# Routed experts of the second half of the tokens, computed only where they are chosen

## The reference, cut to what matters

```python
for e in range(2):                                  # shared experts, all tokens
    shared_out += (silu(x @ s_w1[e].T) * (x @ s_w3[e].T)) @ s_w2[e].T
s = sigmoid([x, t] @ W_router.T)                    # 8 scores per token
topk_idx = top_k(s + bias, 2)                       # 2 of 8 experts
gates_full = ...                                    # zero for 6 of 8 experts
for e in range(8):                                  # routed experts, hidden size 128
    routed_out += gelu(x @ r_w1[e].T) @ r_w2[e].T * gates_full[:, e:e+1]
out = (shared_out / 2 + routed_out) / 4
```

## Time and profile before

| | us |
|---|---|
| median of 3 runs | 550.57 (550.49 to 550.91) |
| span of the profiled execution | 549.0 |
| TensorE busy | 535.7 (98%) |
| VectorE busy | 430.2 (78%) |
| ScalarE busy | 380.4 (69%) |
| GpSimd busy | 197.6 (36%) |
| DMA traffic | 37.35 MB |

### The profile page before, as it was taken

The page is one execution under the profiler, slowest core; times in us unless marked ns, Lnnn a source line. Parts: engine busy times, 40 slices in busy tenths (PEclk is TensorE's granted clock), DMA queues, the critical chain, the costliest instruction groups (busy, mean ns, idle before and its releaser), DMA issues.

```text
span 549.0 us, 10031 instructions
## 1 busy us (share of the span) xinstructions
PE 535.7 (98%) x3309; PEld 464.1 (85%) x3309; DVE 430.2 (78%) x1042; ACT 380.4 (69%) x857; POOL 197.6 (36%) x186
## 2 busy tenths in 40 slices
PE   8999999999999999999999989999999999999997
PEld 7877888887877899999999877789999999987785
DVE  4987655676868888668756259989999999999866
ACT  5567767768766755344553256988988888888965
POOL 4688788888788203939000000010000000000100
DMA  8634305521090302030000000111111111111211
GB/s 290 192 153 159 153 4 229 193 111 44 1 338 11 135 4 80 0 117 21 1 1 0 1 1 1 27 32 21 20 19 22 20 31 35 36 36 41 49 50 38
DMA packets 30226, 37.35 MB, mean 68 GB/s; under 512 B 20096, under 2 KB 23648, under 8 KB 29280
## 3 DMA queue, kind: packets, MB, share of 16 engines
q1 hardware_dynamic: 30176, 36.72, 20.8%
HBM read 30.24 MB, written 2.28 MB: 59 GB/s over the span
## 4 chain that ended last, share of the span: by engine, by line
PE 80%; DVE 13%; ACT 3%; issue 2%; POOL 2%; DVEq 0%; ACTq 0%
PE bank L325 10%; PE bank L1264 10%; PE bank L326 10%; PE bank L327 10%; PE bank L1689 4%; PE bank L1775 4%; PE bank L1679 4%; PE bank L1716 3%; PE bank L1717 3%; PE bank L1332 2%; PE bank L1214 1%; POOL hidden_low L387 1%; PE bank L1764 1%; PE bank L1802 1%; PE bank L1788 1%
## 5 line engine op out<-in xcount | busy, mean ns | idle before, releaser
L387 POOL TENSOR_TENSOR hidden_low<-hidden,hidden_high 128x512 fp32r<-128x512 f32 x72 | 94.5, 1320 | 21.5 <-ACT hidden_high L372 19.3
L2070 POOL CAST h_high<-h 128x256 fp32r<-128x256 f32 x15 | 6.4, 426 | 197.5 <-ACT h L1881 191.1
L468 ACT ACTIVATE bank<-bank 128x512 f32<-128x512 f32 x56 | 32.6, 583 | 30.4 <-PE bank L327 30.1
L472 DVE TENSOR_TENSOR hidden<-bank,big 128x512 f32<-128x512 f32 x56 | 38.5, 687 | 14.3 <-ACT bank L468 13.3
L372 ACT CAST hidden_high<-hidden 128x512 fp32r<-128x512 f32 x70 | 43.1, 615 | 4.4 <-DVE hidden L472 3.1
L325 PE MATMUL bank<-xin_high,sw_high 128*128 128x256 f32 x128 | 43.9, 343 | 0.0
L1716 PE MATMUL bank<-taps_high,q1T 128*128 128x512 f32 x94 | 42.8, 456 | 1.0 <-ACT q1T L1844 0.6
L1717 PE MATMUL bank<-taps_low,q1T 128*128 128x512 f32 x94 | 37.1, 395 | 0.0
L1817 ACT ACTIVATE gates_t<-bank,lstm_b_half 128x128 f32<-128x128 f32 x96 | 28.2, 364 | 12.1 <-PE bank L1689 8.8
L1398 DVE COPY yT<-bank 128x256 f32<-128x256 f32 x32 | 13.5, 423 | 28.9 <-PE bank L1264 28.9
L1679 PE MATMUL bank<-x,lstm_wx 128*128 128x128 f32 x256 | 34.4, 277 | 1.7 <-ACT gates_t L1817 0.9
(11 more groups left out here) (274 smaller groups left out, 1734.8 us busy)
## 6 DMA issues: line engine op xcount, KB each, us to landing
big<-gates_scratch SPq DMA_DIRECT2D x7, 2048.0 KB, 7.6
w<-in_f_w SPq DMA_DIRECT2D x16, 256.0 KB, 5.9
onehot<-topi_scratch SPq DMA_DIRECT2D x8, 512.0 KB, 4.0
outT<-x SPq DMA_DIRECT2D x15, 128.0 KB, 2.1
xT<-in_xT SPq DMA_DIRECT2D x3, 512.0 KB, 6.9
hidden<-in_ffn_w SPq DMA_DIRECT2D x3, 256.0 KB, 5.3
hidden<-in_conv_w SPq DMA_DIRECT2D x3, 256.0 KB, 4.4
xT<-in_xT SPq DMA_DIRECT2D x2, 256.0 KB, 4.0
```

What stands on the lines that cost most here:

```text
L387: pool.tensor_tensor(hidden_hl[u % 3][1][:, :], hidden[u % 3][:, :], hidden_hl[u % 3][0][:, :].bitcast(F32), ALU.subtract).then_inc(s_lo, 1)
L472: dve.tensor_tensor(hidden[u % 3][:, :].rearrange("p (i k) -> p i k", k=P), r_bank[j % 2][:, :].rearrange("p (i k) -> p i k", k=P), gate_r ...
```

## The change

The number of dense chunks becomes 4 (`DENSE`): chunks 0 to 3 are as before. Chunks 4 to 7 (tiles 16 to 31, 2048 tokens, 4096 token-expert pairs) get the shared experts alone, from four new programs `shared_pe`, `shared_act`, `shared_dve` and `shared_sp`; in these the low part of the hidden tile and of x is made on VectorE instead of GpSimd. The pairs of the router are sorted by expert into slots: within chunks 2 and 3 VectorE and TensorE count and place them by prefix sums (`slot_counts` to `slots_experts`), each expert's share filled up to whole tiles of 128 slots, at most `SPARSE_TILES` = 39. GpSimd writes the 4096 rows of x to their slots in DRAM with 32 indirect DMAs (`scatter_pool`), 128 rows of 512 bytes each. Then a new stage, here called the sparse stage, takes the 39 tiles in 13 trios: SyncE reads each tile's expert number from SBUF into a register and loads that expert's two weight matrices by it (`load_weights`), and the trio's rows (`load_xs`); TensorE transposes, and multiplies in plain f32 (`sparse_turn`, `sparse_up`, `sparse_down`, 136 columns since the gate scores are made with the same matmul from weights prepared by `routed_gate_weights`); the results go back to DRAM by slot (`store_y`). Buffers: 5 trios of weights and rows, 2 of results. At last GpSimd fetches the two result rows of each token with 32 further indirect DMAs (`gather_pool`), and VectorE adds them, times the gate, to tokens and scores (`combine`) in the groups 0 and 1 of stage C, 16 instructions a chunk.

Around it: the choice of half 1 becomes two quarters (`CHOICES`), made at the ends of groups 0 and 1, after the combines. The gather of group 0's tokens, `weight_sums` and the first expert splits move from chunk 7 and group 0 into the sparse stage. `prepare_weights` stays behind `gather_pool` in GpSimd's program. Chunk 2 also issues DMAs of 1 MB (rows of x), 2.5 MB (a first fill of the slots, DRAM to DRAM) and 1 MB (weights, DRAM to DRAM). No gate rows are loaded for chunks 4 to 7.

The constants, and what `chunk` issues beside its units in chunks 2 and 3:

```diff
+HALF = NTILE // 2
+PAIRS_ROUTED = HALF * P * 2
+SPARSE_TILES = PAIRS_ROUTED // P + E - 1
+TRIO = 3
+TRIOS = SPARSE_TILES // TRIO
+W_SPARSE = 2 * P + E
+YROW = P + E
...
+        if c == 2 and u == 11:
+            slots_counted()
+        if c == 3 and u == 0:
+            slots_based()
+        if c == 3 and u == 1:
+            slots_placed()
+        if c == 3 and u == 3:
+            slots_gated()
+        if c == 3 and u == 4:
+            slots_experts()
+        if c == 3 and u == 11:
+            store_gate_weights()
+    if c == 2:
+        load_gate_rows(3, 1)
+        sp.dma_start(x_rows[:, :], t["x_rows"]).then_inc(s_rows, 16)
+        some = t["xT"].rearrange("p (a b) -> (p a) b", b=C)
+        sp.dma_start(xs_dram[0:TOK, :], some).then_inc(s_rows, 16)
+        sp.dma_start(xs_dram[TOK:SPARSE_TILES * P, :], some[0:SPARSE_TILES * P - TOK, :]).then_inc(s_rows, 16)
+        sp.dma_start(wcat[:, :, 0:2 * P], t["r_cat"]).then_inc(s_wcat, 16)
+    if c == 3:
+        sp.wait_ge(s_gg, 3 * NRO)
+        sp.dma_start(rw2_rows, t["r_w2"]).then_inc(s_gw, 16)
```

The slots and the shared chunks (`shared_act` does the tanh and the high parts of `chunk`'s ScalarE program, one unit apart):

```diff
+def slot_counts():
+    pe.wait_ge(s_sce, 2)
+    pe.wait_ge(s_id, BEFORE_READY)
+    chosen_rows = rank[:, HALF:NTILE, :].rearrange("p i e -> p e i")
+    for k, w in enumerate((before, ones[:, :])):
+        mm = pe.matmul(by_expert(acc_bank[1][:, k * P:(k + 1) * P]), w, chosen_rows, start=True, stop=True)
+    mm.then_inc(s_side, 1)
...
+def slots_placed():
+
+    first_of = by_expert(scan)[:, :, 0:1].rearrange("p e o -> p (e o)")
+    dve_pos(dve.tensor_tensor(shift, shift, first_of, ALU.subtract))
+    dve_pos(dve.tensor_tensor(scan, scan, earlier, ALU.add))
+    dve_pos(dve.tensor_tensor(by_expert(scan), by_expert(scan),
+                              shift.rearrange("p (e o) -> p e o", o=1).to_broadcast([P, E, HALF]), ALU.add))
+    dve_pos(dve.tensor_tensor(by_tile(placed), by_tile(scan), rank[:, HALF:NTILE, :], ALU.mult))
+    dve_pos(dve.tensor_reduce(pair_at[:, 1, :], by_tile(placed), X, ALU.max))
+    dve_pos(dve.tensor_reduce(pair_at[:, 0, :], by_tile(placed), X, ALU.add))
+    dve_pos(dve.tensor_tensor(pair_at[:, 0, :], pair_at[:, 0, :], pair_at[:, 1, :], ALU.subtract))
+    dve.tensor_copy(slot_at[:, :, :], pair_at).then_inc(s_sided, 1)
...
+def routed_gate_weights():
+    pe.wait_ge(s_sce, 3)
+    pe.wait_ge(s_gw, 32)
+    for e in range(E):
+        mm = pe.matmul(acc_bank[0][:, e * E:(e + 1) * E], rw2_rows[:, e * P:(e + 1) * P], gate_w[:, :],
+                       start=True, stop=True)
+    mm.then_inc(s_side, 1)
...
+def shared_up(k):
+    c, j = k // NSH, k % NSH
+    if j == 0:
+        pe.wait_ge(s_xs, 2 * c + 2)
+    if k < FIRST_SHARED + 2:
+        pe.wait_ge(s_q, k - 1)
+    elif k == FIRST_SHARED + 2:
+        pe.wait_ge(s_gg, DENSE * NRO)
+    else:
+        pe.wait_ge(s_q, k - 2)
+    for b, w in zip(shared_pair(k), (sw1_hl, sw3_hl)):
+        product(b[:, :], w, slice(j * P, (j + 1) * P), x_hl[c % 2], True, True).then_inc(s_ab, 1)
...
+        pe.wait_ge(s_dc, TURNED)
+    pe.wait_ge(s_lo, v + 1)
+    product(acc_bank[c % 2][:, :], sw2_hl, slice(j * P, (j + 1) * P), hidden_hl[v % 3],
+            j == 0, j == NSH - 1).then_inc(s_down, 1)
...
+def shared_silu(k):
+    v = shared_number(k)
+    dve.wait_ge(s_th, k + 1)
+    dve.scalar_tensor_tensor(pb[k % 2][:, :], th[k % 2][:, :], 1.0, shared_pair(k)[0][:, :],
+                             ALU.add, ALU.mult).then_inc(s_p, 1)
+    dve.wait_ge(s_p, k + 1)
+    dve.wait_ge(s_ab, 2 * k + 2)
+    dve.wait_ge(s_lo, v - 2)
+    dve.tensor_tensor(hidden[v % 3][:, :], pb[k % 2][:, :], shared_pair(k)[1][:, :], ALU.mult).then_inc(s_q, 1)
...
+def shared_low(k):
+    v = shared_number(k)
+    dve.wait_ge(s_hi, v + 1)
+    dve.wait_ge(s_lo, v)
+    dve.tensor_tensor(hidden_hl[v % 3][1][:, :], hidden[v % 3][:, :], hidden_hl[v % 3][0][:, :].bitcast(F32),
+                      ALU.subtract).then_inc(s_lo, 1)
...
+def shared_dve():
+    for k in range(FIRST_SHARED, LAST_SHARED):
+        c, j = k // NSH, k % NSH
+        shared_silu(k)
+        if k > FIRST_SHARED:
+            shared_low(k - 1)
+        if j == 0 and c + 1 < NCHUNK:
+            shared_x_low(c + 1)
+        if j == 0 and c > DENSE:
```

The indirect writes and SyncE's program:

```diff
+def scatter_pool():
+    pool.wait_ge(s_sided, SLOTS_READY)
+    pool.wait_ge(s_rows, 48)
+    for i in range(HALF):
+        for r in range(2):
+            pool.indirect_dma_start(xs_dram[:, :], bass.IndirectOffsetOnAxis(slot_at[:, r, i:i + 1], 0),
+                                    x_rows[:, i * C:(i + 1) * C], None).then_inc(s_scat, 16)
...
+def load_weights(m):
+
+    if m >= RING:
+        sp.wait_ge(s_sd, m - RING + 1)
+    for k in range(TRIO * m, TRIO * (m + 1)):
+        e = sp.value_load(tile_expert[0:1, k:k + 1], min_val=0, max_val=E - 1)
+        sp.dma_start(w_ring[k % (RING * TRIO)], wcat[ds(e, 1), :, :].rearrange("o p k -> (o p) k")
+                     ).then_inc(s_trio[m % RING], 16)
...
+def load_xs(m):
+
+    if m >= RING:
+        sp.wait_ge(s_xt, m - RING + 1)
+    rows = xs_dram[m * TRIO * P:(m + 1) * TRIO * P, :].rearrange("(j p) c -> p j c", j=TRIO)
+    sp.dma_start(xs[m % RING].rearrange("p (j c) -> p j c", j=TRIO), rows).then_inc(s_trio[m % RING], 16)
...
+def store_y(m):
+    sp.wait_ge(s_yv, m + 1)
+    rows = ys_dram[m * TRIO * P:(m + 1) * TRIO * P, :].rearrange("(j p) c -> p j c", j=TRIO)
+    sp.dma_start(rows, y_out[m % 2].rearrange("p (j c) -> p j c", j=TRIO)).then_inc(s_yst[m % 2], 16)
...
+    for c in range(DENSE, NCHUNK):
+        load_expert(c)
+    sp.wait_ge(s_wcat, 32)
+    sp.wait_ge(s_gg, DENSE * NRO)
+    sp.wait_ge(s_sided, EXPERTS_READY)
+    for m in range(RING):
+        load_weights(m)
+    choice_store(0)
...
+def sparse_sp():
+    sp.wait_ge(s_scat, 16 * 2 * HALF)
+    sp.wait_ge(s_down, DENSE_UNITS)
+    for m in range(RING):
+        load_xs(m)
+    sp.wait_ge(s_vc, 32)
+    for k in range(2):
+        gather_loads(0, k)
+    load_slots(0)
+    load_raw_weights()
+    for m in range(TRIOS):
+        if m + RING < TRIOS:
+            load_xs(m + RING)
+            load_weights(m + RING)
+        store_y(m)
```

The sparse stage, the indirect reads and the sum:

```diff
+def sparse_turn(m):
+    pe.wait_ge(s_trio[m % RING], TRIO_LOADED * (m // RING + 1))
+    if m < 2:
+        pe.wait_ge(s_q, LAST_SHARED)
+    else:
+        pe.wait_ge(s_xc, m - 1)
+    for j in range(TRIO):
+        mm = pe.transpose(bank[m % 2][:, j * P:(j + 1) * P], xs[m % RING][:, j * P:(j + 1) * P], ident[:, :])
+    mm.then_inc(s_xt, 1)
...
+def sparse_up(m):
+    pe.wait_ge(s_xc, m + 1)
+    if m >= 2:
+        pe.wait_ge(s_sg, m - 1)
+    for j in range(TRIO):
+        w = w_ring[(TRIO * m + j) % (RING * TRIO)]
+        mm = pe.matmul(bank[4 + m % 2][:, j * P:(j + 1) * P], w[:, 0:P], x_cols[m % 2][:, j * P:(j + 1) * P],
+                       start=True, stop=True)
+    mm.then_inc(s_su, 1)
...
+def sparse_down(m):
+    pe.wait_ge(s_sg, m + 1)
+    if m >= 2:
+        pe.wait_ge(s_yv, m - 1)
+    for j in range(TRIO):
+        w = w_ring[(TRIO * m + j) % (RING * TRIO)]
+        mm = pe.matmul(bank[2 + (m + 1) % 2][:, j * YROW:(j + 1) * YROW], hid[m % 3][:, j * P:(j + 1) * P],
+                       w[:, P:W_SPARSE], start=True, stop=True)
+    mm.then_inc(s_sd, 1)
...
+def sparse_pe():
+    sparse_turn(0)
+    sparse_turn(1)
+    sparse_up(0)
+    for m in range(TRIOS):
+        if m + 2 < TRIOS:
+            sparse_turn(m + 2)
+        if m + 1 < TRIOS:
+            sparse_up(m + 1)
+        sparse_down(m)
...
+def sparse_gelu(m):
+    act.wait_ge(s_su, m + 1)
+    if m >= 3:
+        act.wait_ge(s_sd, m - 2)
+    act.activation(hid[m % 3], bank[4 + m % 2][:, 0:TRIO * P], ACT.Gelu).then_inc(s_sg, 1)
...
+def sparse_y(m):
+    act.wait_ge(s_sd, m + 1)
+    if m >= 2:
+        act.wait_ge(s_yst[m % 2], 16 * (m // 2))
+    act.copy(y_out[m % 2], bank[2 + (m + 1) % 2][:, 0:TRIO * YROW]).then_inc(s_yv, 1)
...
+def gather_pool():
+    y_stored(pool, TRIOS - 1)
+    for c in range(DENSE, NCHUNK):
+        if c >= DENSE + 2:
+            pool.wait_ge(s_comb, 2 * (c - DENSE - 1))
+        for i in range(TILES_CHUNK):
+            tile = (c - DENSE) * TILES_CHUNK + i
+            for r in range(2):
+                pool.indirect_dma_start(y_rows[c % 2][:, r, i, :], None, ys_dram[:, :],
+                                        bass.IndirectOffsetOnAxis(slot_at[:, r, tile:tile + 1], 0)
+                                        ).then_inc(s_yg[c % 2], 16)
...
+def combine(c):
+    dve.wait_ge(s_yg[c % 2], 16 * 2 * TILES_CHUNK * ((c - DENSE) // 2 + 1))
+    dve.wait_ge(s_ct, c + 1)
+    dve.wait_ge(s_sce, c + 1)
+    for r in range(2):
+        if r:
+            dve.wait_ge(s_comb, 2 * (c - DENSE) + 1)
+        for i in range(TILES_CHUNK):
+            tile = c * TILES_CHUNK + i
+            y, g = y_rows[c % 2][:, r, i, :], slot_gate[:, r, tile - HALF:tile - HALF + 1]
+            dve.scalar_tensor_tensor(score[:, tile, :], y[:, P:YROW], g, score[:, tile, :], ALU.mult, ALU.add)
```

(16 more changed lines are left out.)

556 lines of the change are left out of this document (356 added, 200 removed).

## The result

| | before | after |
|---|---|---|
| time, median of 4 runs | 550.66 us (550.49 to 550.91) | 602.44 us (601.76 to 603.73) |
| ratio, 95% interval | | 1.0936 (1.0915 to 1.0956) |
| span of the profiled execution | 549.0 us | 600.4 us |

The account below looks back on a forecast made before the run. TensorE was taken to bound the kernel before 183.68 us. 549.0 + 2.5 (chunks 2 and 3) - 37 (chunks 4 to 7) + 42.5 (sparse stage) + 4 (stage C) = 561.0 us span, 562.6 us median; range 541 to 597.

Parts of the forecast that it names:

- What bounds the kernel: Before 183.68 us TensorE is the bound; work taken off it counts in full until another engine or queue becomes the bound.
- Chunks 2 and 3: Slot counting and gate weights added to these chunks: +2.5 us, with the added DMAs hidden.
- 0.4 us, between 0 and 3: Chunks 2 and 3: what VectorE's some 28 small slot steps cost beyond the lead of 3 units.
- Chunks 4 to 7: Shared experts only: 82.2 us becomes 45, -37 us, ends 42 and 50, with VectorE as the new bound.
- The indirect writes: GpSimd's 32 writes beside chunks 4 to 7: 1.2 us each from 103 us, ended at 143, hidden.
- The turning point of 1.4 us: Cost of one indirect write at which the cover by chunks 4 to 7 is gone.
- GpSimd is slow: Rival, chance 0.15: indirect DMAs from 1.4 us each delay the sparse stage; at 2.0 us each, 594.6 us in all.
- The sparse stage: New stage of 13 trios: SyncE's queue at 4.6 us a trio sets 46 us in all, +42.5 us net.
- The quick SyncE: Rival, chance 0.20: cheap register reads leave the sparse stage to TensorE and the DMAs, 29 us; 544.5 us in all.
- Stage C: Groups 0 and 1 with VectorE's combine and choices: VectorE about full, +4 us, between 0 and 12.
- The shared port: Rival, chance 0.15: VectorE's steps in groups 0 and 1 hold up indirect reads, 1.7 us each; 572.6 us in all.
- The range: Whole kernel: 541 to 597 us without the outer tenths; the ends of all terms give 535 to 600.

Follow-up runs that it names:

- e6: Changed kernel with VectorE's slot steps in chunk 3 spread over more units, the gate ones moved to the start of the sparse stage; 595.3 us.
- e13: Changed kernel with twice GpSimd's descriptor memory (2048 bytes a partition) and a wait for landing after every 4 indirect writes; 599.6 us.
- e2: Changed kernel with each tile's expert fixed in the program, so SyncE reads no register; all loads stay; 587.5 us.
- e3: Changed kernel with each late trio's third weight load and all result stores moved from SyncE's to ScalarE's queue; 590.1 us.
- e9: Changed kernel with plain SyncE reads instead of the 32 indirect reads, behind the loads of group 1's tables; choice by slot left out; 594.5 us.
- e10: Changed kernel with the combination of routed results done for only one tile of four in each chunk; 595.9 us.
- e5: Changed kernel with half of GpSimd's descriptor memory, 512 instead of 1024 bytes a partition; 614.3 us.
- e1: Changed kernel with twice GpSimd's descriptor memory, 2048 instead of 1024 bytes a partition, nothing else; 628.4 us.
- e16: Changed kernel with twice GpSimd's descriptor memory and no indirect writes, so the sorting of rows is left out; 600.5 us.
- e12: Changed kernel with the 32 indirect writes replaced by 32 plain SyncE DMAs of the same bytes; sorting by slot left out; 588.5 us.

## Why the prediction was wrong

The direction was right (slower had 0.75), and the largest loss that it names, SyncE's queue in the sparse stage, came about as forecast. The sum was 39.4 us too low, by several steps that failed each for itself: the slot steps of VectorE in chunk 3, taken for nearly hidden; the indirect writes, taken for wholly hidden; the two ends of the sparse stage; and stage C, where only the load of VectorE was asked about.

**What bounds the kernel** held: with TensorE's 44 us of routed products gone, chunks 4 to 7 went from 82.2 us to 48.0.

**Chunks 2 and 3** (+2.5 forecast, 9.9): the failed step is "0.4 us, between 0 and 3" for VectorE's insertions. I priced 28 steps at 0.2 to 0.3 us and took its 16 us of free time for room. They were some 12 us; five of them, 0.88 to 1.47 us each, stood beside GpSimd's large steps, the exclusion that the earlier trace rows shows and that I used for another rival only. TensorE idled 3.5 us, most of it from 85 to 91, and ran at the 1.2 GHz level (matmuls of 512 columns every 0.43 us instead of 0.23) from 91.2 to 97.8. With the steps spread out the first write came 3.9 us earlier, and the kernel took 7.1 us less (e6).

**Chunks 4 to 7** (45, ends 42 and 50; measured 48.0) held. VectorE was at 0.83 and TensorE at 0.87, not over 0.9 and 0.8. Where GpSimd disturbs nobody they are 4.7 us shorter, 43.3, below my 45, and there VectorE is the bound as forecast (35.62 of 37.40 us in e13). One wait was not in the sum: the copy of the gate weights stands ahead of VectorE's first shared step, whose tanh was ready at 108.8, and waits for TensorE's products behind chunk 3:

```profile
113.30 0.23 DVE L686 COPY big<-bank 128x64 f32<-128x64 f32 x1 [5.07 <-PE bank L680]
```

**The indirect writes** (hidden, forecast; 8.0 us of waiting measured): the price of one, 1.27 us against 1.2, was good. Its pauses, which make it 1.6, and the start at 111.4 instead of 103 were not in the sum, and nor were 5.1 us from the last write to the first turn (the landing, an issue and the load of the first rows). The turning point of 1.4 us was right and was passed; the rival *GpSimd is slow* names the mechanism, at 1.6 instead of its 2.0 us.

**The sparse stage** (46; 51.0): SyncE's 4.6 us a trio was measured as 4.6 (4.75 with the first two), and e2 and e3 show that this queue sets the stage. Two errors cancel in it: a read is cheaper than forecast, and some 0.3 us a trio go elsewhere. Too small were the two ends: the first of the 8 late loads came 6.5 us into the stage, not 3, and after the last one 9.0 us went by, not 6. The first waits for the first down product, and TensorE came to that at a low clock after its wait for the rows: 0.57 was granted from 167.4 to 174.0, and the six instructions of a trio's up products took 1.28 us instead of the 0.67 of those at 212.3. The five steps from 167.75 to the end of that down product took 5.5 us; with the durations seen at the full level they would take some 3 (an estimate). A read with its address steps costs 0.64 us, 1.11 from load to load less 0.47 for the issue; my 0.75 was near. The Trainium skill ("DMA: Bandwidth & Descriptors", section Latency and other measured facts) has about 600 ns as a floor for a tensor load. The 0.64 lie near it, though the load by itself is recorded with 0.27 us. The quick SyncE, which I gave 29 us, takes 35.8 (e2).

**Stage C** (+4, ends 0 and 12; 14.9 in groups 0 and 1 alone): the failed step is the question whether VectorE is full. Its load in group 0 was about as forecast, 29.57 us, but the group took 41.14. What I left out is that others start late beside the indirect reads, some 5 to 6 us (e9), and that the combination costs some 6 though VectorE has room (e10). 3 to 4 us in the groups and 3.5 behind them stay open.

**The shared port** is refuted as the rival had it (1.7 us a read): 24 of the 32 reads took 0.94 to 0.98 us, the longest 1.41, and 24 of the 32 writes 0.96 or 0.97 beside VectorE's two-input steps, the longest 1.47; what is above the shortest is 2.0 and 1.9 us in all. By the Trainium skill's rule ("SBUF — State Buffer", section SBUF: two separate sides) GpSimd would be the one that waits; in these runs ScalarE and SyncE wait too, which the rule doesn't cover.

**The range** missed by 5.4 us: five terms came out above their values, all with one sign, three of them through GpSimd, while I had taken their ends as independent.

## What to carry over

Work that TensorE is freed from must be paid for in queues: count the instructions that each queue has to issue for one unit of the new work, the steps ahead of its first unit and behind its last, and the way from the last write to the first use. Small steps on an engine with free time aren't free where the next engine waits for what stands behind them. Terms that hang on the same engine miss together, so their ends belong in the range together.

## What the runs showed of the hardware

- An indirect DMA of 128 rows costs GpSimd 0.96 us and a gap of 0.30. In the writes it stands still for about 1.8 us or more after every 3, 7, or 14, with 512, 1024 or 2048 bytes a partition for its descriptors (e5, the changed kernel, e1).
- While a run of them goes on, instructions of VectorE and ScalarE may begin 2 to 12 us after what they wait for, and SyncE's register steps can take 0.7 us instead of 0.02 to 0.15 (e1, e16); e13's 32 reads in a row are the exception. With plain DMAs of the same number and size chunks 4 to 7 took 37.4 us (e12) and groups 0 and 1 71.4 (e9). What the engines share there stays open; the traces speak against DMA bandwidth (a share of 0.36 in e1's chunks 4 to 7) and against the loading of instructions (3 packets there, of 1.2 us at most).
- Twice the memory for descriptors made the kernel slower by 26 us (e1); with a wait after every 4 writes the same memory gave 599.6 us (e13). So in the writes it is the missing pauses, not the memory itself.
